# Second layer's tiles 0 and 1 begun in the third and last chunk of the FFN, and TensorE's and ScalarE's programs written out without loops

## What is computed

```python
x = x + L0_xattn(layernorm(x), ctx, Wq, bq, Wkv, bkv, Wo, bo)   # 32 heads of 128, 8 kv heads
x = x + L0_ffn(layernorm(x), gate_w, up_w, down_w, fc1_w, fc2_w, expert_w, gamma, beta)
x = x + L1_xattn(layernorm(x), ctx, wq, wk, wv, wo, ln_w)       # inside: rmsnorm; 32 heads of 16, 8 kv heads
x = x + L1_ffn(layernorm(x), W_gate, b_gate, W_e, b_e)          # top 2 of 8 experts

def L0_ffn(h):
    r = sum of the two largest of (h @ gate_w)
    shared = relu(h @ up_w)**2 @ down_w                  # 512 -> 1024 -> 512
    routed = ((h @ fc1_w) @ expert_w * r) @ fc2_w        # 512 -> 256 -> 256 -> 512
    return layernorm(shared + routed, gamma, beta)

def L1_ffn(h):
    y = relu(h @ W_e[e] + b_e[e]) for the top two e of (h @ W_gate + b_gate)
    return mean of the two
```

## Time and profile before

| | |
|---|---|
| median of 3 runs | 1885.27 us (1885.04 to 1886.22) |
| the profiled execution | 1885.55 us, span of its instructions 1883.8 us |
| PE busy | 1781.2 us, 95% |
| DVE, ACT, POOL busy | 1236.2, 900.6, 495.4 us |
| granted TensorE clock, mean | 0.986 |

### The profile page before, as it was taken

How to read it: one execution, slowest core, us unless ns; L and a number is a source line. 1 busy time by engine, 2 the same in 40 slices (tenths; PEclk the granted TensorE clock), 3 DMA queues, 4 the chain that set the end, 5 groups by cost and what they waited for, 6 DMA issues and landing times. The chain is left out here.

```text
span 1883.8 us, 36264 instructions
## 1 busy us (share of the span) xinstructions
PE 1781.2 (95%) x14128; PEld 983.3 (52%) x14128; DVE 1236.2 (66%) x2288; ACT 900.6 (48%) x1433; POOL 495.4 (26%) x370
## 2 busy tenths in 40 slices
PE   5989999999999999999999999977999999999997
PEld 2545555555555555555555444443555555555553
DVE  6785565646565646566566577758777877877863
ACT  5544444343434343434444333243666666666662
POOL 0161832505207034076000000000223322322324
PEclk9989999999999999999999999989999999999999
DMA  5011220301204012034100300004100000000000
GB/s 229 23 45 46 86 95 23 124 2 69 79 1 143 4 47 101 1 112 147 57 2 1 118 1 1 0 11 170 51 7 7 7 13 7 7 13 7 7 12 12
DMA packets 18376, 88.79 MB, mean 47 GB/s; under 512 B 2608, under 2 KB 2864, under 8 KB 10160
## 3 DMA queue, kind: packets, MB, share of 16 engines
q1 hardware_dynamic: 18224, 86.58, 12.7%
HBM read 65.60 MB, written 20.97 MB: 46 GB/s over the span
## 5 line engine op out<-in xcount | busy, mean ns | idle before, releaser
L642 PE MATMUL bank<-R 128*128 128x512 f16 (+1 forms) x7152 | 1304.7, 341 | 23.7 <-issue 7.1
L642 PEld LDWEIGHTS bank<-R 128*128 128x128 f16 x7152 | 584.4, 99 | 659.7 <-issue 40.9
L1490 DVE SCALAR_TENSOR_TENSOR R<-bank,biases,R 128x512 f16<-128x512 f32 x288 | 204.6, 746 | 249.8 <-ACT R L1095 209.0
L505 POOL TENSOR_TENSOR R<-R 128x512 f32<-128x512 f32 x112 | 156.2, 1395 | 430.2 <-ACT R L1286 428.9
L1095 ACT ACTIVATE R<-bank,biases 128x512 f16<-128x512 f32 x128 | 87.7, 686 | 235.2 <-PE bank L642 234.5
L396 POOL TENSOR_SCALAR R<-R 128x2048 f32<-128x2048 f32 (+1 forms) x20 | 33.8, 1692 | 435.9 <-PE bank L642 377.2
L1286 ACT ACTIVATE R<-R,msk 128x512 f32<-128x512 f32 x128 | 90.5, 717 | 49.3 <-DVE R L1824 49.3
L1502 DVE SCALAR_TENSOR_TENSOR R<-bank,R 64x512 f16<-64x512 f32 x64 | 44.0, 688 | 100.2 <-ACT R L1103 99.7
L1575 DVE SCALAR_TENSOR_TENSOR X<-bank,X 128x512 f32<-128x512 f32 x128 | 86.8, 683 | 34.7 <-PE bank L642 34.6
L642 PE MATMUL bank<-CT,R 128*128 128x512 f16 x384 | 91.6, 390 | 17.1 <-DVE CT L1464 11.8
L1824 DVE SCALAR_TENSOR_TENSOR R<-bank,R 128x512 f32<-128x512 f32 x128 | 87.1, 681 | 29.3 <-PE bank L642 28.3
(11 more groups left out here) (148 smaller groups left out, 2022.4 us busy)
## 6 DMA issues: line engine op xcount, KB each, us to landing
R<-in_wB SPq DMA_DIRECT2D x16, 1024.0 KB, 6.0
R<-in_wX SPq DMA_DIRECT2D x16, 1024.0 KB, 5.0
w_split<-AW SPq DMA_DIRECT2D x16, 1024.0 KB, 4.8
R<-w_split SPq DMA_DIRECT2D x12, 1024.0 KB, 7.2
R<-in_ctxT SPq DMA_DIRECT2D x4, 1024.0 KB, 10.0
X<-in_x SPq DMA_DIRECT2D x4, 1024.0 KB, 13.6
out<-X SPq DMA_DIRECT2D x16, 256.0 KB, 2.4
R<-in_wB SPq DMA_DIRECT2D x7, 512.0 KB, 5.6
```

The source lines that it names most:

```text
L505: g.tensor_tensor(acc, acc, tmp[:, e % 2, :], ALU.add).then_inc(e_acc, 1)
L642: last = pe.matmul(dst, a(sa), b(sb_), start=(k == 0), stop=(k == m - 1))
L1490: v.scalar_tensor_tensor(out=dst, in0=src, scalar=bias, in1=hi, op0=ALU.add, op1=ALU.subtract).then_inc(done, 1)
```

## The change

Four parts.

1. **Tile 0 moves one chunk forward.** Its norm, turn, projection and the turning of its heads go from `ffn_last` (the fourth chunk) into the third one (`ahead = c == 2`), between the jobs and downs there. In `ffn_last` its scores, softmax and weighing of V stand after jobs 2, 5, 7, 8, 10 and 11. Since two tiles now go through counted semaphores earlier, `attn_stat`, `attn_turn`, `chunk_first`, `tile_root` and `chunk_root_of` number them anew.
2. **Tile 1 moves forward.** It gets places of its own (`TILE1`), is normed during the last chunk's jobs, projected between its downs, and both its scores are taken before the last FC2. Its softmax stays in `attn_step(1)`.
3. **The last FFN tiles' finishing moves back.** `y_stats`, `y_norm` and `y_add_to_x` of tile 14, and `y_of` and all of these of tile 15, go into `attn_step(1)` on DVE. Tile 15 is held in a buffer of its own (`y_last`).
4. **No loops on TensorE and ScalarE.** `Fori` becomes Python's `range` in the first attention, the FFN and the second layer. VectorE, GpSimd and SyncE keep their loops, except the FFN's on VectorE.

SyncE's order follows: the expert biases come in four transfers, and expert 7's weights wait for `f_add` of all 16 tiles, since `y_last` lies in their place.

```diff
+            if isinstance(n, int) and n < 2:
+                return (TILE0, TILE1)[n]
@@ SyncE
             expert(0)
             sp.wait_ge(a_y, 1)
-            sp.dma_start(R3, be.broadcast_to([P, NE * D])).then_inc(be_in, 16)
+            bias_rows(0)
             sp.wait_ge(n_lo, ffn_stat(0) + 1)
             expert(1)
+            sp.wait_ge(b_s, 4)
+            bias_rows(2)
+            bias_rows(6)
             sp.wait_ge(f_mm, 2 * NT)
-            for e in (2, 3, 6, 7):
+            for e in (2, 3, 6):
                 expert(e)
+            sp.wait_ge(b_t, 4)
+            bias_rows(4)
+            sp.wait_ge(f_add, NT)
+            expert(7)
@@ TensorE
-            with pe.Fori(0, 3) as i:
+            for i in range(3):
                 for k in range(8):
...
                 for q in range(12):
                     ffn_job(c, q)
+                    if ahead and q == 6:
+                        tile_turn(pe, attn_turn(0), 0, 4, attn_turn(0))
+                    if ahead and q == 8:
+                        for arrived in (wq_in, wkv_in, wo_in, g1_in):
+                            pe.wait_ge(arrived, 16)
+                        pe.wait_ge(f_y, c * TC)
+                        project(0, ctx_tile(0), T20)
...
                 ffn_job(c, 8)
+                weigh_v(0, 0)
                 ffn_job(c, 9)
-                scores(0, 1)
                 ffn_job(c, 10)
-                turn_p(0, 0)
+                turn_p(0, 1)
                 ffn_job(c, 11)
-                weigh_v(0, 0)
+                weigh_v(0, 1)
                 ffn_down(c, 0)
+                pe.wait_ge(g_top, NC)
+                turn_o(0)
+                tile_turn(pe, attn_turn(1), 1, 0, attn_turn(1))
                 ffn_fc2(0)
-                turn_p(0, 1)
+                project(1, ctx_tile(1), T20)
                 ffn_down(c, 1)
-                weigh_v(0, 1)
+                output(0)
@@ ScalarE
                 job(c, 9)
+                norm_root(act, attn_stat(1), 1)
+                out_hi(0, 0)
                 job(c, 10)
-                turned_p(0, 0)
+                tile_hi(act, attn_stat(1), 1, TILE1.yn)
+                turned_p(0, 1)
                 job(c, 11)
@@ VectorE, ffn_chunk
+                    if ahead and q == 2:
+                        norm_stats(dve, attn_stat(0), 0, x_tile(0), True)
+                    if ahead and q == 5:
+                        norm_apply(dve, attn_stat(0), 0, x_tile(0), TILE0.yn)
+                    if ahead and q == 6:
+                        tile_lo(dve, attn_stat(0), 0, TILE0.yn)
+                    if ahead and q == 11:
+                        q_lo(0)
+                        kv_lo(0)
@@ VectorE, attn_step
+                if two:
+                    less_max(n, 0)
+                else:
+                    y_stats(NT - 2)
...
                 if two:
                     expert(n - 2, 7)
+                else:
+                    y_of(NC - 1, TC - 1)
                 less_max(n, 1)
+                if not two:
+                    y_norm(NT - 2)
+                    y_add_to_x(NT - 2)
                 if one:
                     mask_of(n - 1)
```

More of the change, by code:

```diff
@@ L1230, in _ @@
                 b_step(s, 0, (s + 1) // NC, False, (s + 2) * TC if s < 2 else None)
-            with act.Fori(0, 3) as i:
+            for i in range(3):
                 for k in range(8):
@@ L1274, in ffn_chunk @@
                 store(3)
+                if ahead:
+                    turned_q(0)
                 y_root(c * TC + 2)
+                if ahead:
+                    turned_k(0)
             def norm_store(n, buf):
@@ L1361, in attn_step @@
                     expert(n - 1, 0)
+                if not two:
+                    y_root(NT - 1)
+                if one:
                     expert(n - 1, 1)
@@ L1390, in ffn_last @@
                 job(c, 1)
[L1391 removed]
                 job(c, 2)
[L1393 removed]
                 job(c, 3)
[L1395 to L1402 removed]
                 act.wait_ge(w_lo, LAST_CONV)
                 exponentials(0, 0)
+                for q in range(4, 8):
+                    job(c, q)
@@ L1430, in _ @@
-            ffn_chunk(0)
-            with act.Fori(1, NC - 1) as c:
+            for c in range(NC - 1):
                 ffn_chunk(c)
@@ L1434, in _ @@
             attn_step(1, 1)
-            with act.Fori(0, 6) as i:
+            for i in range(6):
                 for k in range(2, 4):
@@ L1916, in attn_step @@
                 probs_lo(n, 1)
+                if not two:
+                    y_stats(NT - 1)
                 if one:
@@ L1923, in attn_step @@
                     expert(n - 1, 1)
+                if not two:
+                    y_norm(NT - 1)
+                    y_add_to_x(NT - 1)
                 if has(n, -2):
@@ L1980, in ffn_last @@
                 reciprocals(0, 1)
-                norm_stats(dve, attn_stat(1), 1, x_tile(1), True)
+                job(c, 10)
+                tile_lo(dve, attn_stat(1), 1, TILE1.yn)
+                job(c, 11)
+                out_scale(0, 1)
+                norm_stats(dve, attn_stat(2), 1, x_tile(2), True)
+                out_lo(0, 1)
                 y_of(c, 0)
                 y_stats(c * TC)
-                norm_apply(dve, attn_stat(1), 1, x_tile(1), rel[:, 1, :])
+                norm_apply(dve, attn_stat(2), 1, x_tile(2), yn2)
@@ L1985, in ffn_last @@
                 y_norm(c * TC)
-                tile_lo(dve, attn_stat(1), 1, rel[:, 1, :])
+                q_lo(1)
                 y_add_to_x(c * TC)
-                out_scale(0, 1)
-                out_lo(0, 1)
+                kv_lo(1)
+                tile_lo(dve, attn_stat(2), 1, yn2, attn_turn(1) + 1)
+                add_out(0)
                 y_of(c, 1)
                 y_stats(c * TC + 1)
-                norm_stats(dve, attn_stat(2), 1, x_tile(2), True)
+                norm_apply(dve, ffn_stat(0), 0, x_tile(0), TILE0.yn)
@@ L2004, in ffn_last @@
-                norm_apply(dve, ffn_stat(0), 0, x_tile(0), TILE0.yn)
-                tile_lo(dve, ffn_stat(0), 0, TILE0.yn, attn_turn(1))
-                y_of(c, 3)
-                y_stats(NT - 1)
-                y_norm(NT - 1)
-                y_add_to_x(NT - 1)
-            ffn_chunk(0)
-            with dve.Fori(1, NC - 1) as c:
+                less_max(1, 0)
+            for c in range(NC - 1):
                 ffn_chunk(c)
```

217 lines of the change are left out of this document (111 added, 106 removed).

## The result

| | before | after |
|---|---|---|
| median | 1885.74 us (1885.04 to 1887.3, 4 runs) | 1867.22 us (1865.91 to 1869.07, 4 runs) |
| the profiled execution, its span | 1885.55, 1883.8 us | 1866.54, 1864.8 us |
| granted TensorE clock, mean | 0.986 | 0.991 |

The ratio is 0.9901, 95% interval 0.9884 to 0.9919: 18.5 us faster. The forecast of 1872 was 4.8 us too high, and inside its range (1860 to 1880).

The account below looks back on a forecast made before the run. PE, busy 95%, bounds the kernel, so only its pauses and low clock can give time. Gains of 5.2 us idle, 2.3 clock and 5.7 loops make 13.2: span 1870.6, median 1872 us, range 1860 to 1880 (own range 1866 to 1878).

Parts of the forecast that it names:

- Loops: Unlooped PE and ScalarE gain 5.7 us: 3.9 in the first attention, 1.7 in the second layer.
- The step on which this hung: First attention's two round borders: VectorE keeps its loop, its 1.66 us issue wait costs PE 1.5 us at each.
- Rival D: Loops give nothing, because code in line is late now and then: 1885 us, chance 0.04.
- Third chunk: With tile 0 moved in, PE pauses 4.6 us for 0.8 before, 2.5 of it at the turn behind job 6.
- Last chunk: PE waits 9.1 us in the last FFN chunk, 5.2 of it before `weigh_v(0, 1)` for ScalarE's `turned_p`.
- the five that the prediction lists: PE's small waits in the last chunk before `weigh_v(0, 1)`: 0.2, 0.6, 1.1, 0.8 and 0.6 us.
- VectorE's sum over the chunk: VectorE limits the last chunk: its last low half comes at 42.7 us at the earliest, 44.6 by the walk.
- `attn_step(1)`: PE waits 7.6 us in tile 1's attention step: 1.3, 3.8 before tile 2's turn, 1.4, 0.8 and 0.3.
- Clock: Low clock behind the 5.2 and 3.8 us pauses costs 2.8 and 1.7: 4.5 us for 6.8, 2.3 gained.
- Rival B: Pauses around the third and last chunks only move, clock as before, only the loops gain: 1879.5 us, chance 0.17.
- Rival A: The walk stacks overlapping waits; the chunks and step keep some 6 us idle, no low clock: 1852 us, chance 0.13.
- C: Slower: small waits hold the clock low through the last chunk's twelve jobs and first down: 1893.7 us, chance 0.04.

Follow-up runs that it names:

- experiment 2: The changed kernel with VectorE's two loops written out too: 1864.87 us, ratio 0.9884.
- Experiment 1: The kernel before with only TensorE's and ScalarE's loops written out: 1878.78 us, ratio 0.9956.
- experiment 4: The changed kernel with ScalarE's `turned_p(0, 1)` right behind job 9, ahead of tile 1's root, `out_hi` and job 10: 1865.67 us, ratio 0.9887.
- experiment 6: The changed kernel with tile 11's last norm operations and add on 8 of 512 columns, about 2.1 us less VectorE work early in the last chunk: 1865.91 us.
- Experiment 3: The changed kernel with VectorE's gate logits of tile 0 ahead of tile 14's norm and add in `attn_step(1)`: 1866.98 us, ratio 0.9894.
- experiment 9: experiment 2 with, in the last chunk, ScalarE's `turned_p(0, 1)` behind tile 1's root and VectorE's low half of tile 1 and gate sums behind job 11: 1859.27 us.
- experiment 11: experiment 9 with tile 14's norm and add and tile 15's statistics, norm and add further back on VectorE in `attn_step(1)`: 1859.55 us, ratio 0.9858.
- experiment 12: experiment 11 with tile 1's norm, low half and gate sums, and tile 15's statistics and add, later, and tile 0's turn one job later: 1854.41 us.
- experiment 7: The changed kernel with the edits of experiment 2 and experiment 4 together: 1863.10 us, ratio 0.9875.
- experiment 8: experiment 2 with tile 0's turn in the third chunk one job later on TensorE, behind job 7: 1864.10 us, ratio 0.988.
- experiment 10: experiment 2 with VectorE's norm and add of tile 14 behind the second probabilities' low half in `attn_step(1)`: 1863.22 us, ratio 0.9887.

## Why the prediction came out as it did

**Loops: right.** 3.9 us predicted for the first attention, 4.2 in the trace; 1.7 for the second layer, 1.7 there. The step on which this hung, that VectorE's own border takes back 1.5 us at each of two, is shown by after's pauses (1.48, 1.44) and by experiment 2 (3.4 us at the two borders for the 3.0). Experiment 1 gives the loops by themselves 7.0 us by the starts for the 5.7 predicted, the same 4.2 and 1.8 among them, and 7.5 by the medians. Rival D is out.

**Third chunk: 4.6 us of pauses predicted, 4.2 found.** The turn waits 1.66 for 2.5, the first down 0.99 (0.30 + 0.69) for 0.9, the next turn 0.53 for 0.8, the small one 1.00 for 0.4.

**Last chunk: 9.1 us predicted, 7.3 found.** The pause before `weigh_v(0, 1)`, 5.2, came as 4.86, at the named engine and operation. Counted from job 0's first matmul (about 1219.0, thirty matmuls into the group that starts at 1212.51), PE is through with it at 41.5 us for 42.1, had done job 11 at 36.7 for 36.9, and the last low half comes at 44.0 for 44.6. The small ones are 2.4 us together, not 3.9; and the five that the prediction lists add up to 3.3, so 0.6 of its 9.1 had no place. No down waits. The size was right, and of the two reasons given one: the place of `turned_p` in ScalarE's list (experiment 4 moves the pause), not VectorE's sum over the chunk (experiment 6 leaves it). The Trainium skill (TensorE: Matmul & The Clock Gate, section Architectural detail: the array is 16× 32×32, not 1× 128×128) has ScalarE and VectorE strictly first in, first out. This trace agrees: in after PE was through with the second `turn_p` at 1253.07, and ScalarE's `turned_p`, which only had to read it, began at 1258.54, behind job 10 and `tile_hi` in its list.

**`attn_step(1)`: 7.6 us predicted, 4.1 found.** This is the term that was mis-sized, and 3.5 us of the miss. The named pause came (3.16 for 3.8), and the first was 0.57 for 1.3. But the 1.4 us at `weigh_v(1, 1)` and 0.3 are missing, and `turn_q` waits 0.38 for 0.8. Experiment 3 shows where they went. There PE ran at the full clock, and waited 1.30 us at `weigh_v(1, 1)`, 0.58 at the turned outputs, 0.62 at `turn_q`: 2.5 us, just the sum predicted. In after PE runs 2.5 us late by the low clock, and the three waits shrink to 0.38. The sum had counted both, the waits as if PE ran at full speed and the clock's loss as if nobody waited behind it. They lie on top of each other: where another engine is the limit, PE's low clock is paid out of PE's own waiting. The 34.7 us that three kernels take behind the pause, at 2.5, 1.2 and 1.7 us of low clock, say the same.

**Clock: 4.5 us of loss predicted, 4.6 found**, 2.0 + 0.1 behind 4.86 and 2.5 behind 3.16; no low clock behind 1.66. That the sums agree is luck: 2.8 was predicted behind the pause at the weighting and 2.1 found, 1.7 behind the other and 2.5 found. Behind the same 4.86 us pause the 24 matmuls of the first down took from 6.61 to 7.66 us in seven kernels, 1.3 to 2.3 over the full-clock price, and behind the 3.16 us one the twelve took from 3.42 to 4.92, 0.7 to 2.2 over it. That long pauses bring low clock was read rightly from the earlier trace rows; a price to a tenth can't be had from one row.

**The sum**: 13.2 us of span predicted, 19.0 found. Of the missing 5.8, 0.9 stood in the traces ahead of the first border, 0.3 is at the borders, and 4.8 in the two chunks and the step (12.3 for 7.5); the rest is rounding. In these 12.3 the idle time fell by 10.8 us for the 5.2 predicted, and PE's busy time, at the higher clock, by 1.5 for 2.3. Of the idle time that the prediction kept and the kernel did not, 3.5 us are in the step, 2.1 of them the double count (waits of 2.5 us of which 0.38 showed), 1.8 in the last chunk and 0.4 in the third: pauses priced a little high. So the time came inside the range by its width; of what the tiles were moved for, the idle time, about half the gain was forecast.

Rival B (pauses only moved) is out: the named pauses of these stages fell from 26.5 us to 15.6. Rival A was right in its kind, in that the walk stacked waits which overlap, but not in its size, since the two long pauses and their clock stood. C is out: in after the low clock came only behind the two long pauses, not behind the small ones.

## What to carry to other kernels

When an engine that releases the bottleneck works through a fixed list, ask of each long pause which instruction is at the head of the list and why, not how full the engine is: reordering a few calls gave 7.5 to 10.5 us here with no work removed, and taking 1.8 us of work away early in the chunk left the pause untouched. Don't add the low clock behind a pause to waits that follow close behind it; where the waits are for an engine that is late anyway, its lateness covers both. And a loop is only gone when the engines that feed its neighbour have lost theirs too.

## What the runs showed of the hardware

- **The same pause, two clocks.** Before the first down PE paused 1.97 us in experiments 9, 11 and 12, and in 9 and 11 the program is the same up to there. The windows of the first 5.1 to 5.2 us behind it (length, busy PE, PEld, DVE, ACT, POOL, granted clock) in experiment 9:

```profile
1254.90:1260.00 5.10, 5.10 (x24) 2.21 (x24) 4.06 (x16) 1.14 (x3) 1.09 (x3) 1.00 0.75 316
```

  and in experiment 11:

```profile
1255.30:1260.50 5.20, 5.20 (x17) 2.06 (x18) 4.14 (x16) 1.17 (x3) 1.09 (x3) 0.67 0.69 287
```

  Full clock once and a mix of 1.2 and 2.4 GHz the other time, 1.7 us on 24 matmuls (5.34 and 7.03). In the step it went so too: 3.16 us before tile 2's turn brought low clock in after (4.76 us for twelve matmuls), 3.17 us before `turn_p(1, 1)` in experiment 3 none (1.07 us, the full-clock price). Pauses of 2 to 3 us can't be priced to better than that from one profiled execution.
- **The same end, two lengths.** Behind `turn_p` of tile 15 all kernels run the same 61 us, with pauses of 1.47 us before a weighting and 2.00 us before the last gate. In eight profiled executions, before and after among them, no low clock follows; in six (experiments 1, 2, 7, 8, 9 and 11) it costs 1.5 to 1.7 us, behind the 1.47 us pause in experiments 1 and 11 (4.44 us for 2.75) and behind the 2.00 us one in the others. Experiment 2, and then experiment 10, which is ordered otherwise in `attn_step(1)` alone:

```profile
1831.93 0.46 PE L672 MATMUL bank<-g1w,R 128*128 128x8 f16 x12 [2.00 <-ACT R L621]
1832.24 22.57 PE L672 MATMUL bank<-R 128*128 128x512 f16 x96
...
1833.69 0.46 PE L672 MATMUL bank<-g1w,R 128*128 128x8 f16 x12 [2.00 <-ACT R L621]
1834.00 20.88 PE L672 MATMUL bank<-R 128*128 128x512 f16 x96
```

- **A pause for issue without a loop.** In experiment 12 PE stood 1.06 us at 1324.74 for nothing that the profile names. The 1 MB of expert 7's weights, issued at 1319.87, lands 4.8 us later, in the same tenth of a microsecond; the program waits for it only one expert later. Whether code in line came late behind this transfer stays open: no run separates the two, and after, with the same transfer, has no such pause. The DMA view doesn't settle it. The queues for instructions moved nothing from 1303 to 1325.5 us, and one packet falls between 1325.50 and 1325.75, when PE was running again; such a packet also falls 0.3 to 0.7 us behind each of the four pauses at PE's loop borders in before, but in experiment 11 one falls at the same time with no pause.
- **The cost of a border on each engine**: PE 2.95 and 2.45 us, VectorE 1.66 us, of which the pipeline passed on 1.5.
